# Second attention in slots of four heads, with the score shift of 12 of 32 heads moved to GpSimd

## The reference

```python
q = (x @ wq.T).reshape(B, S, 32, 8).transpose(0, 2, 1, 3)     # k and v alike
scores = jnp.einsum('bhqd,bhkd->bhqk', q, k) / scale
scores = scores + _rel_bias(rel_pos, S)[None, None]           # one S x S bias for all heads
attn = jax.nn.softmax(scores, axis=-1)
ctx = jnp.einsum('bhqk,bhkd->bhqd', attn, v)
return ctx.transpose(0, 2, 1, 3).reshape(B, S, 256) @ wo.T
```

## Time and profile before

| what | value |
|---|---|
| median of the runs shown | 952.79 us |
| profiled execution, its own time | 953.87 us |
| its span, first to last instruction | 951.8 us |
| mean granted TensorE clock | 0.978 |
| TensorE busy (matmul) | 866.0 us, 91% |
| VectorE busy | 702.3 us, 74% |
| ScalarE busy | 687.0 us, 72% |
| GpSimd busy | 261.3 us, 27% |
| the second attention | from 366.1 us (first scores) to about 735 us |

### The profile page before, as it was taken

One profiled execution on the slowest core, in us unless ns is written; L12 is line 12 of the kernel. 1 busy time (PEld: TensorE's weight loads), 2 busy tenths in 40 slices (PEclk: granted clock), 3 DMA queues, 4 the chain that ended last, 5 costly groups with the idle time before them and its releaser, 6 DMA issues.

```text
span 951.8 us, 20997 instructions
## 1 busy us (share of the span) xinstructions
PE 866.0 (91%) x7200; PEld 711.0 (75%) x7200; DVE 702.3 (74%) x2130; ACT 687.0 (72%) x1538; POOL 261.3 (27%) x360
## 2 busy tenths in 40 slices
PE   3777899999999998999999999999998998999994
PEld 2556778788888887676777776767666987899994
DVE  6888878878875557888888989898987462365447
ACT  2778857768676337999999999999998322366646
POOL 0345542322343120200202021111112256334432
PEclk8889999999999999999999999999999999999998
DMA  6203021110010012010202020202021212244534
GB/s 200 67 1 98 15 79 62 40 35 13 13 45 13 24 34 61 21 28 1 70 2 70 1 70 2 69 1 59 10 66 48 86 62 94 73 109 124 133 136 174
DMA packets 54760, 54.85 MB, mean 58 GB/s; under 512 B 17953, under 2 KB 48929, under 8 KB 54658
## 3 DMA queue, kind: packets, MB, share of 16 engines
q1 hardware_dynamic: 51250, 44.18, 16.0%
q0 software_dynamic: 3408, 9.34, 2.8%
HBM read 32.85 MB, written 20.65 MB: 56 GB/s over the span
## 4 chain that ended last, share of the span: by engine, by line
PE 50%; DVE 19%; ACT 18%; issue 8%; DMA 2%; POOL 1%; another core or an unknown queue 1%; DVEq 0%; ACTq 0%; SPq 0%; POOLq 0%
PE ps L445 11%; PE ps L447 9%; PE ps L446 9%; PE ps L969 5%; ACT G L1492 4%; ACT G L1502 4%; ACT wu_rows L1492 3%; PE ps L986 3%; PE ps L957 2%; PE ps L677 2%; PE ps L692 2%; DVE G L2037 2%; ACT RT L1252 1%; PE ps L750 1%; DVE wu_rows L2037 1%
## 5 line engine op out<-in xcount | busy, mean ns | idle before, releaser
L1492 ACT ACTIVATE G<-G,small 128x256 f32<-128x256 f32 x296 | 133.7, 517 | 7.0 <-DVE small L2037 7.0
L445 PE MATMUL ps<-WU 128*128 128x256 f32 x384 | 117.4, 306 | 17.3 <-DVE wu_rows L1859 6.7
L2037 DVE CUSTOM_DVE_ANT_0 G<-ps,nb 128x256 f32<-128x256 f32 x296 | 111.6, 419 | 20.7 <-PE ps L957 17.8
L1502 ACT COPY G<-ps 128x512 f32<-128x512 f32 x192 | 113.3, 590 | 9.6 <-PE ps L969 9.5
L2398 POOL TENSOR_SCALAR_AFFINE_SELECT G<-G 128x256 f32<-128x256 f32 x128 | 76.3, 619 | 145.8 <-ACT G L1337 145.6
L446 PE MATMUL ps<-WU 128*128 128x256 f32 x384 | 108.7, 283 | 0.0
L447 PE MATMUL ps<-WU 128*128 128x256 f32 x384 | 108.6, 283 | 0.0
L1492 ACT ACTIVATE wu_rows<-wu_rows,small 128x256 f32<-128x256 f32 x216 | 98.1, 518 | 3.2 <-DVE small L2037 3.2
L969 PE MATMUL ps<-ident,G 128*128 128x128 f32 x592 | 92.6, 283 | 4.6 <-ACT G L1502 3.3
L2037 DVE CUSTOM_DVE_ANT_0 wu_rows<-ps,nb 128x256 f32<-128x256 f32 x216 | 81.6, 419 | 14.6 <-PE ps L957 13.4
L445 PEld LDWEIGHTS ps<-WU 128*128 128x128 f32 x384 | 73.1, 190 | 25.8 <-DVE WU L1865 9.5
(11 more groups left out here) (251 smaller groups left out, 2354.5 us busy)
## 6 DMA issues: line engine op xcount, KB each, us to landing
xs<-G SPq DMA_DIRECT2D x8, 645.0 KB, 6.5
G<-xs SPq DMA_DIRECT2D x39, 128.0 KB
G<-x SPq DMA_DIRECT2D x17, 256.0 KB, 3.4
G<-in_x SPq DMA_DIRECT2D x16, 256.0 KB, 2.8
wu_rows<-yy SPq DMA_DIRECT2D x8, 512.0 KB, 7.6
x<-G SPq DMA_DIRECT2D x15, 256.0 KB, 2.4
wu_rows<-in_wu SPq DMA_DIRECT2D x8, 384.0 KB, 5.7
wraw<-in_wu SPq DMA_DIRECT2D x8, 256.0 KB, 2.9
```

What stands on the lines that cost most here:

```text
L445: pe.matmul(o, lh, rh, start=start, stop=False, skip_group_check=True)
L1492: m = act.activation(p, p, ACT.Exp, scale=-1.0, bias=mneg[:, k:k + 1])
L1502: act.copy(probT(h), halves(2 + h % 2)).then_inc(probT_act, 1)
L2037: m = dve.tensor_tensor_reduce(prob(H2 * i + h)[:, t, :], ps[:, SCORE_BANKS[(H2 * i + h) % 3], S * t:S * (t + 1)], nbv[:, t, :], 1.0, -FMI ...
```

## The change

An iteration is now eight slots of four heads (`QUADS`). In each slot TensorE computes the scores of four heads with 8 matmuls into four banks (0, 1, 5, 6), and waits before them until VectorE has dealt with all four heads of the slot before. Then it transposes the four heads of the slot before, in two pairs with dense work between and behind them. `mix` runs for eight heads at a time, in slots 1, 3, 5 and 7, ahead of the transposes. As four banks now hold scores, the dense work has lost banks: everything dense shares bank 7 and bank 4, and bank 4 is also the one that `mix` writes. So `qk(i+1, 0)` of slot 4 leaves its result in bank 4, and the mix of slot 5 waits until both parts of the split have read it.

`POOL_SHIFTS` gives how many heads of each slot (2, 2, 1, 2, 1, 2, 1, 1: twelve of 32) skip the exponential in SBUF. For these GpSimd forms p * -1 + mneg in place, TensorE transposes that, and ScalarE's copy out of PSUM becomes an Exp activation. ScalarE now takes all 32 heads; VectorE takes none. GpSimd's three weight splits of an iteration now stand in slots 2, 4 and 6, behind the shifts of the slot, and the norm's root in slot 6.

```diff
-PE2 = dict(heads=(26, 30, 2, 5), x_turn=6, qk=(14, 18), c_turn=(8, 10, 12, 15), ct_turn=17, v=10,
...
-SCORE_BANKS = (0, 1, 5)
-MIX_BANK = 4
+QUADS = H2 // 4
+SCORE_BANKS = (0, 1, 5, 6)
+SHARED_BANK, DENSE_BANK = 4, 7
+POOL_SHIFTS = (2, 2, 1, 2, 1, 2, 1, 1)
...
             if f == 2:
-                return 6
+                return (DENSE_BANK if t else SHARED_BANK) if b else 6
...
+                def scores(i, q):
...
+                        pe.wait_ge(biased_ready, 4 * (QUADS * i + q))
...
                     for t in range(2):
-                        for n in (h, h + 1):
-                            j, g = n % 4, n // 4
+                        for j in range(4):
                             r = slice(32 * j, 32 * j + 32)
...
+                def turn(n):
+
+                    quad, j = divmod(n, 4)
+                    if j < POOL_SHIFTS[quad % QUADS]:
+                        pe.wait_ge(prob_shifted, shifts(n))
+                    else:
+                        pe.wait_ge(prob_ready, n + 1 - shifts(n))
+                    if n >= 2:
+                        pe.wait_ge(probT_taken, n - 1)
...
+                        if q == 5:
+                            if left:
+                                pe.wait_ge(split_hi[2], 8 * (i + 1) + 4)
+                                pe.wait_ge(split_ready[2], 4 * (i + 1) + 2)
+                            pe.wait_ge(o_copied[2], 4 * i + 1)
+                            mix(i, 1)
...
+                        before = H2 * i + 4 * q - 4
+                        if before >= 0:
+                            turn(before)
+                            turn(before + 1)
...
+                        if q == 6 and left:
                             pe.wait_ge(split_ready[2], 4 * (i + 1) + 4)
+                            turned(QS, DENSE_BANK, 0)
...
+                def exponential(n):
+
+                    act.wait_ge(biased_ready, n + 1)
...
+                def take(n):
+
+                    act.wait_ge(probT_turned, n + 1)
...
+                    if n % 4 < POOL_SHIFTS[n // 4 % QUADS]:
+                        act.activation(probT(n), halves(2 + n % 2), ACT.Exp).then_inc(probT_taken, 1)
+                    else:
+                        act.copy(probT(n), halves(2 + n % 2)).then_inc(probT_taken, 1)
...
+                        for j in range(POOL_SHIFTS[q], 4):
+                            exponential(H2 * i + 4 * q + j)
+                        if q in (4, 5) and left:
+                            hi_parts(i + 1, q - 4)
...
+            def shifted(n):
+
+                pool.wait_ge(biased_ready, n + 1)
+                for t in range(2):
+                    k = 2 * (n % 8) + t
+                    p = prob(n)[:, t, :]
+                    m = pool.tensor_scalar(p, p, -1.0, mneg[:, k:k + 1], ALU.mult, ALU.add)
+                m.then_inc(prob_shifted, 1)
```

More of the change, by code:

```diff
@@ L406, in raw_count, with shifts @@
             return 16 * sum(dmas(n) for n in range(load + 1))
[L408 to L422, removed]
+        def shifts(n):
+            quad, j = divmod(n, 4)
+            return (sum(POOL_SHIFTS) * (quad // QUADS) + sum(POOL_SHIFTS[:quad % QUADS])
+                    + min(j + 1, POOL_SHIFTS[quad % QUADS]))
         blk = ctx.enter_context(nc.Block())
@@ L668, in heads @@
             def heads(f, b, n):
[L670 removed]
+                for src, bank, out in ((QS, B_QT[f], heads_q[f]), (KS, b_kt(b, n) if f == 2 else B_KT0, heads_k[f])):
                     w = src.bitcast(F32).rearrange("p (t g c) -> p t g c", t=2, g=8)
@@ L944, in phase2, with turned @@
                 n = iterations[2]
[L946 to L952, removed]
+                def turned(src, bank, group):
+                    w = src.bitcast(F32).rearrange("p (t g c) -> p t g c", t=2, g=8)
+                    for g in range(2):
+                        for t in range(2):
+                            m = pe.transpose(ps[:, bank, S * g + P * t:S * g + P * (t + 1)], w[:, t, 2 * group + g, :], ident[:])
+                    m.then_inc(heads_turned[2], 1)
@@ L976, in mix @@
                         pe.wait_ge(vp_ready[2], i + 1)
[L977 to L988, removed]
+                    pe.wait_ge(probT_taken, H2 * i + 8 * g + 8)
@@ new lines, in mix @@
+                    for quad in (2 * g, 2 * g + 1):
+                        for kt in range(2):
+                            for j in range(4):
+                                h = 4 * quad + j
+                                at = (D2 + 1) * h
+                                m = pe.matmul(ps[32 * j:32 * j + 32, SHARED_BANK, S * (quad % 2):S * (quad % 2 + 1)],
+                                              vp[:, kt, at:at + 32], probT(h)[:, kt, :], start=kt == 0, stop=kt == 1,
+                                              skip_group_check=True, tile_position=(0, 32 * j))
@@ new lines, in one @@
+                        if q == 1:
+                            pe.wait_ge(heads_q[2], 4 * i + 4)
+                            turned(KS, DENSE_BANK, 3)
+                        if q == 2 and not first:
+                            c_turn(2, i - 1, 1, 8)
+                        if q == 3 and not first:
+                            c_turn(2, i - 1, 3, 8)
+                        if q == 4 and left:
+                            pe.wait_ge(heads_q[2], 4 * i + 4)
+                            pe.wait_ge(heads_k[2], 4 * i + 4)
+                            pe.wait_ge(o_copied[2], 4 * i + 1)
+                            qk(2, i + 1, 0)
@@ L1525, in phase2 @@
                 passes(n, one)
-                for h in range(H2 - TURN_LAG, H2):
-                    if on_act(h):
-                        take(n - 1, h, False)
+                for h in range(H2 - 4, H2):
+                    take(H2 * (n - 1) + h)
             def moe():
```

338 lines of the change are left out of this document (195 added, 143 removed).

## The result

| what | before | after |
|---|---|---|
| median | 953.58 us (4 runs) | 999.61 us (4 runs) |
| ratio of after to before | | 1.0478, 95% interval 1.0462 to 1.0494 |
| span of the profiled run | 951.8 us | 998.5 us |
| mean granted TensorE clock | 0.978 | 0.944 |

The change makes the kernel 46 us slower. Forecast were 980 us, with 945 to 1003 as the range. The direction and the two waits came as forecast; the size of the clock term did not.

The account below looks back on a forecast made before the run. The prediction took TensorE and ScalarE as full, VectorE near. From 953.9 us it added 18 for seven longer iterations, took off 3.5 for the last and added 12 for the clock: 980 us, range 945 to 1003.

Parts of the forecast that it names:

- clock term: Second attention: half clock after 14 waits loses 1.7 us each, 24 us if all count; half taken, 12 us.
- Work by engine: One iteration of the second attention: ScalarE 42.7 to 36.7 us, VectorE about 40 to 35.5, TensorE 41.5 to 38.
- Four row groups: TensorE's scores: a slot's eight matmuls overlap in four row groups and cost 0.43 us, saving 3.4 us an iteration.
- Rival C: TensorE's scores: four row groups overlap no better than two, +0.43 us a slot, +21 us, 1001 us; chance 0.05.
- rival B: GpSimd's shifts: late at 1.40 us a product, 6.4 us more an iteration, about +50, 1030 us; chance 0.05.
- Take with Exp: ScalarE's copy out of PSUM with Exp: 0.46 us like a plain copy; upper end 4.2 us more.
- First wait: Slot 5: TensorE's mix waits for bank 4 until slot 4's product is split, standing 4.5 us.
- Second wait: Slot 6: TensorE's transposes of the split queries wait for the second split, standing 3.6 us.
- Smaller waits: Slots 0, 3 and 4: TensorE's transposes and mix wait 1.4, 0.4 and 0.9 us, about 3 us together.
- Period at full clock: One iteration of the second attention: 38 + 4.5 + 3.6 + 3 = 49.1 us against 46.5.
- Rival A: Slots 5 and 6: the waits are covered and lighter work decides, period 41 us, time 910 us; chance 0.15.
- Two engines are full.: Second attention before the change: TensorE busy 44.4 and ScalarE 43.7 of 46 us, so both bound it.

Follow-up runs that it names:

- split_early: Changed kernel with the split's product, high parts and low parts moved earlier in the engines' lists, same work and banks: 926.30 us, ratio 0.9713 to the kernel before.
- slot4_alone: Changed kernel with only the slot 4 part of split_early (first product, its high and low parts early): 967.32 us, ratio 1.0134 to the kernel before.
- slot5_alone: Changed kernel with only the slot 5 part of split_early (high parts behind one exponential, ahead of the second takes): 968.07 us, ratio 1.0120 to the kernel before.
- filled: Changed kernel with 14 and 12 matmuls that nobody reads ahead of the two waits for the split: 971.97 us, ratio 1.0190 to the kernel before.
- shifts_alone: Kernel before, in its own order, with 12 of 32 heads shifted on GpSimd and its splits spread out: 965.18 us, ratio 1.0103 to the kernel before.
- hi_first: Changed kernel with ScalarE's high parts of the split ahead of the slot's exponentials in slots 4 and 5: 959.12 us, ratio 1.0063 to the kernel before.

## Why the prediction was right, and where it was off

- Work by engine. Forecast for an iteration were 36.7 us for ScalarE, 35.5 for VectorE, 38 for TensorE as pitches. The busy rows of split_early, where neither wait distorts them, have 38.2, 35.4 and 39.3 in 42 us. The step is right. (Two calls of high parts stand in the sum with 2.1 us, where the 1.21 read for one gives 2.4; it stands there before and after alike.)
- Four row groups. Taken as 0.43 us a slot, measured 0.44. The estimate by the Trainium skill's 3.07 for four row tiles ("TensorE: Matmul & The Clock Gate", Part 3), 0.56, is not borne out for these matmuls of 256 columns; the measurement decides. Rival C falls with it, although its 1001 us was nearer to the measured time than my 980: the time alone would have spoken for the wrong cause.
- GpSimd. 0.46 us taken, 0.48 measured; rival B falls. VectorE's bias steps average 0.419 us in both profiles, as the row at 547.60 had said. The Trainium skill's rule of shared SBUF interfaces ("GPSIMD Engine Reference", section 1) speaks of VectorE instructions with two SBUF inputs; this one has one, and the trace agrees that it is not lengthened. "Nobody should wait for it" did not hold quite: the weight loads did, 4.9 us in all.
- Take with Exp. 0.46 us taken, the price of a copy; the means are 606 and 599 ns, so the 4.2 us of the upper end did not come.
- First wait. Worked out as 4.5 us, measured 4.3 in six of seven iterations and 3.8 in the first. Right. Removing it alone (slot4_alone) brings 32 us.
- Second wait. 3.6 worked out, 3.4 measured. Right, and shown to be separate by slot5_alone.
- Smaller waits. About 3 us an iteration forecast; all others of TensorE's list add up to 23 us over the eight. Right in sum.
- Period at full clock. 49.1 worked out, 48.9 in filled, whose 972 us stands against the sum's 968. Right.
- Clock. This is the term that was mis-sized. I took 14 waits x 1.7 us x one half = 12 us, with 24 as the upper end. Filled shows 27.6 us: every wait brought the lower level, and in each iteration it lasted about twice as long behind one of the two as the gap in rows 8 had shown. That makes 15.6 of the 19.6 us between 980 and 999.6; the other 4 are the difference between 968 and 972.
- Rival A, that the waits are covered, did not come, and its price was too low: without both waits I had a period of 41 and 910 us; split_early has 42.3 and 926. With only the first covered I had 44.6 and 940, with no clock term for the wait that stays; slot4_alone has 47.8 and 967.
- "Two engines are full." Of the kernel before this was a reading of busy shares. The 8.7 us for which TensorE waited for ScalarE there, and shifts_alone, speak for TensorE alone as the bound. It did no harm to the forecast, since neither wait hung on it. It did to the next one: for the shift alone I expected 930 to 944 and got 965, in part perhaps through the late root.

The order of sizes: the slots and the shift together are worth -28 us (split_early against before). The place of the split in the engines' lists, with the two waits that it makes, is worth +73.

## What to carry to other kernels

Where a bank is shared between a side chain and the main path, count the side chain from its last release on the main path to the end of its last reader, through each engine's list in order; if that is longer than what the waiting engine has ahead of the wait, the difference is lost once in every pass, and moving the chain's instruction up in the list is free (two swapped statements were worth 40 us here). Add the clock to waits of TensorE's: here waits of 4.3 and 3.4 us in each iteration brought 3.9 us more through the clock, and with waits of 2.4 and 1.8 us (hi_first) it fell in three of seven iterations. A lighter engine brought nothing where the bound one had waited for it only 1.3 us an iteration; read that wait, and try the relief alone, before building an order on it. And work moved to an idle engine stands in that engine's list: look at who waits for what now stands behind it, as for the root in shifts_alone.

## What the runs showed of the hardware that was not expected

- By the records, TensorE seems to start matmuls of different row groups out of the order of the list (inferred, as the records name no group): with groups 0, 1, 0, 1, 2, 3, 2, 3 in the list, four start within 0.1 us and the eight take 0.44 us from the start to the next instruction, as with 0, 1, 2, 3, 0, 1, 2, 3.
- The lower clock level after a wait has two lengths. In the iteration shown it lasted from about 551.7 to 555.1 with the wait of 4.3 us and from about 561.9 to 568.8 with the shorter one of 3.4 us. In the next iteration it was the other way round: about 602.9 to 609.7 with the first, 616.5 to 619.9 with the second. So the length of the wait does not decide it; what does is open.
- Matmuls whose result nobody reads, 26 in an iteration, saved 27.6 us. With them the granted clock of an iteration is 1.00, where it was 0.90.
